# A two-direction Mamba block: groups of 128 channels over all 1024 tokens, one ring of ten slots written in place, and a second set of states prepared by token

## The reference, cut to what matters

```python
xz = einsum(h, W_in); x, z = halves          # 256 channels each
x = silu(causal_conv(x, 4 taps) + conv_b)
dt, B, C = split(einsum(x, Wx))              # rank 64, 16 states, 16 states
dt = softplus(einsum(dt, Wdt) + bdt)
dA = exp(dt * A)                             # token x channel x state
dBx = (dt * x) * B
h_t = dA_t * h_(t-1) + dBx_t ; y_t = sum over states of h_t * C_t
y = (y + x * D) * silu(z); out = einsum(y, W_out)
```

## Time and profile before

| what | value |
|---|---|
| runs | 877.89 and 879.49 us |
| span of the profiled execution | 875.2 us, so 2.7 to 4.3 us of a run's time lie around a span |
| DVE busy | 796.6 us, 91% |
| POOL busy | 794.2 us, 91% |
| ACT busy | 654.4 us, 75% |
| PE matmul busy | 644.4 us, 74% |
| mean granted TensorE clock | 0.878 |
| moved | 108.12 MB, mean 124 GB/s |

### The profile page before, as it was taken

The page is one execution under the profiler, slowest core; times in us unless marked ns, Lnnn a source line. Parts: engine busy times, 40 slices in busy tenths (PEclk is TensorE's granted clock), DMA queues, the critical chain, the costliest instruction groups (busy, mean ns, idle before and its releaser), DMA issues. The chain is left out here.

```text
span 875.2 us, 9930 instructions
## 1 busy us (share of the span) xinstructions
PE 644.4 (74%) x2650; PEld 262.4 (30%) x2650; DVE 796.6 (91%) x816; ACT 654.4 (75%) x1147; POOL 794.2 (91%) x391
## 2 busy tenths in 40 slices
PE   8577786967778795867787795878788696568474
PEld 5232231413333231313333231323333131223223
DVE  3379999999999999999999999999999999999866
ACT  3588787877879787876888787876888786865514
POOL 0398999999998999999998999999998999998925
PEclk9989796979989798979889798989989897966778
DMA  3885746474765745583775656484675557385003
GB/s 68 173 191 108 160 97 144 87 160 79 174 137 121 168 88 119 97 185 76 153 163 109 152 93 135 84 190 93 130 162 107 121 104 154 75 180 181 25 0 97
DMA packets 82103, 108.12 MB, mean 124 GB/s; under 512 B 43648, under 2 KB 56960, under 8 KB 81792
## 3 DMA queue, kind: packets, MB, share of 16 engines
q1 hardware_dynamic: 82048, 107.49, 57.6%
...
## 5 line engine op out<-in xcount | busy, mean ns | idle before, releaser
L582 POOL TENSOR_TENSOR dbx<-step_rep,bc_rep 128x1024 f32<-128x1024 f32 x192 | 452.5, 2379 | 14.6 <-DMA step_rep<-step 12.1
L835 ACT ACTIVATE da_ps<-step_rep,neg_a 128x512 f32<-128x512 f32 x384 | 257.7, 690 | 95.5 <-DVE hs L1109 94.5
L592 POOL TENSOR_TENSOR ch<-hs,bc_rep 128x1024 f32<-128x1024 f32 x120 | 284.9, 2375 | 19.9 <-DVE hs L1109 15.3
L1109 DVE TENSOR_TENSOR_SCAN hs<-da_ps,dbx 128x512 f32<-128x512 f32 x192 | 220.5, 1204 | 24.4 <-ACT da_ps L835 12.0
L1109 DVE TENSOR_TENSOR_SCAN hs<-da_ps,carry,dbx 128x512 f32<-128x512 f32 x192 | 232.6, 1264 | 5.9 <-ACT da_ps L835 5.9
L1369 PE MATMUL y_ps<-ch,stack 128*32 128x512 f32 x1024 | 158.1, 693 | 91.4 <-POOL ch L592 53.2
L761 ACT ACTIVATE dbx_tok<-c_ps,b_cols 128x256 f32<-128x256 f32 x256 | 111.0, 489 | 27.2 <-PE c_ps L1421 22.4
L1360 PE MATMUL c_ps<-x_dbl,select 128*128 128x512 f32 x160 | 105.2, 745 | 33.7 <-DVE ch L1020 27.0
L1020 DVE TENSOR_TENSOR ch<-hs,c_ps 128x2048 f32<-128x2048 f32 x56 | 126.6, 2261 | 0.0
L1308 PE MATMUL pre<-h_t,w_conv 128*128 128x512 f32 x248 | 113.6, 600 | 7.5 <-ACT xs L713 5.8
L1433 PE MATMUL da_ps<-ident,dbx_tok 128*128 128x128 f32 x512 | 76.6, 284 | 33.6 <-DVE hs L1109 32.4
...
## 6 DMA issues: line engine op xcount, KB each, us to landing
step_rep<-step SPq DMA_DIRECT2D x256, 256.0 KB, 5.4
...
```

Of the source, the lines that this page charges most:

```text
L582: nc.gpsimd.tensor_tensor(dbx[:, j % DBX_RING], dtx_rep[:, r], b_rep[:, s % 2, k, :].unsqueeze(1).to_broadcast([P, 2, CHUNK]), ALU.mult).t ...
L592: nc.gpsimd.tensor_tensor(ch[:, n % RING], hs[:, n % RING], c_rep[:, s % 2, k, :].unsqueeze(1).to_broadcast([P, 2, CHUNK]), ALU.mult).then ...
L835: nc.scalar.activation(bank, dt_rep[:, r, e, :], ACT.Exp, scale=neg_a[:, half_of(unit), 2 * (unit % 2) + e, g, k:k + 1]).then_inc(da_ready, 1)
L1109: nc.vector.tensor_tensor_scan(in_scan_order(hs[:, n % RING, e, :], s), in_scan_order(factor, s), in_scan_order(term, s), initial, ALU.mul ...
```

## The change

A group is now **128 channels of one direction over all 1024 tokens**. The scan of a unit is one instruction of 128 x 1024 instead of two of 128 x 512, and starts from zero: there is no kept state. There are again 4 groups for each batch and 16 units in a group, four **places** of four units, one place for each quad. A direction is two groups. This text numbers the units of a direction 0 to 31: 0 to 15 are its first ("even") group, 16 to 31 its second ("odd") one.

`ring` has ten slots of 128 x 1024. A slot holds `dBx` (or, for a unit by token, the decay), then the scan's result, then the product with C, all in place. A slot is free again when PE has summed the whole place of its last unit (`wait_slot`). PSUM has two sets of 1024 columns (`SETS = 2`, `s_ps`) in place of three banks of 512.

By token are now units 12 to 15 and 16 to 19 (quad 3 for both groups, `scale_both`, 32 instructions of 256 columns for each direction, as many as before) and units 28 to 31 (quad 2 of the odd group, `scale_one`, 32 instructions of 128 columns, new). B by token is turned round on PE (`turn_b`); the small transfers are gone. POOL makes C products for units 8 to 19 and 28 to 31, DVE for 0 to 7 and 20 to 27, as two instructions of 4 x 512 columns for each place (`times_c`): one after the place's last scan, one after the scan behind it.

```diff
-RING = 4
+RING = 10
+SETS = 2
-B_AHEAD = 3
-DA_BANKS = 3
-STATE_QUADS = (((0, 1, 2, 3), (0, 3, 1, 2)),) * NG
-TOKEN_QUADS = ((3,),) * NG
-DA_SLOTS = 4
-DBX_RING = 4
-POOL_C = ((0, 1, 3, 8, 9, 12, 13),
...
+QUADS = ((0, 1, 2, 3), (3, 0, 1, 2))
+TOKEN_PLACES = ((3,), (0, 3))
+POOL_C_PLACES = ((2, 3), (0, 3))
...
+CONVOLVE = {0: (0, 5, 7, 11), 2: (3, 5, 8, 11)}
+SILU_AT = 13
+X_DBL = (14, 15)
+SOFTPLUS_AT = 7
+DTX_AT = (8, 9)
...
+EXPS_AFTER = ((2, 3, 4, 5, 6, 7, 8, 9, 10, 11, 13, 14, 15, 16, 17, 18),
+              (3, 4, 5, 5, 6, 7, 8, 9, 10, 11, 13, 14, 15, 16, 16, 17))
+B_FIRST = 2
+B_AFTER = ((3, 4, 5, 6, 7, 9, 10, 11, 12, 12, 12, 12, 12, 12, 13, 13),
+           (1, 2, 2, 3, 4, 5, 6, 7, 8, 8, 8, 8, 9, 9, 10, 10))
+BOTH_TAKEN = (14, 1, 5, 9)
+BOTH_SCALED = {(1, 15): (0, 0, 4), (0, 0): (0, 4, 8), (0, 1): (1, 0, 4), (0, 2): (1, 4, 8),
+               (0, 5): (2, 0, 4), (0, 6): (2, 4, 8), (0, 9): (3, 0, 4), (0, 10): (3, 4, 8)}
...
+            def scan(b, s, n):
+
+                i = unit(b, s, n)
+                dve.wait_ge(da_ready, i + 1)
+                slot = ring[:, i % RING, :]
+                factor, term = s_ps[:, i % SETS, :], slot
+                if by_token(s, n):
+                    dve.wait_ge(dbx_ps, tokens_turned(b, s, n) + 1)
+                    factor, term = slot, factor
...
+            def turn_tokens(b, s, n):
...
+                pe.wait_ge(scanned, i - SETS + 1)
```

More of the change, by code:

```diff
@@ L22 @@
 FAR = QUAD // NEAR
-UNITS = STATES // QUAD * INNER // BLOCK // 2
-TRANSPOSE_REV, COPY_REV = (4, 5), (5, 6)
-FIRST_STAGES = {"silu": 10, "x_dbl": 13}
-LATER_STAGES = {"copy x_dbl": 0, "u0": 1, "u1": 2, "take u0": 2, "take u1": 3, "softplus": 5, "dtx": 7}
-CONVOLVE = (7, 7, 8, 8)
-CONVOLVE_READ = 8
-PROJECTIONS = {"z0": 6, "z1": 6, "z2": 3, "z3": 6, "h0": 3, "h1": 4}
-PROJECTIONS_READ = {"z0": 6, "z1": 6, "z2": 5, "z3": 7, "h0": 4, "h1": 6}
-CLOSING = {"save": 3, "start sum": 3, "gate": 2, "output": 4, "residual": 5, "mean": 6, "deviation": 6,
-           "scale": 8, "keep": 9, "transpose": 10, "affine": 13, "largest": 15}
@@ new lines, in take_step @@
+            def take_step(d, j):
+                place, c = j // 2, j % 2
+                g = d % 2
+                a = half_at(g, place)
+                wait_filled(act, "step", d, j)
+                if j == 0:
+                    for r in range(BLOCKS):
+                        act.wait_ge(dt_in[r], FAR * 16 * 2 * d)
+                    wait_dtx(act, d - 1, 1)
+                nc.scalar.activation(step[:, a, 0, columns(c)], pre[:], ACT.Identity, bias=bdt[:, g, a:a + 1]).then_inc(pre_taken, 1)
@@ L692, in copy_z, with softplus @@
+            def softplus(d):
+                nc.scalar.preload_act_table_set(SOFTPLUS)
+                for place in range(2):
+                    wait_taken(act, "step", d, 2 * place + 1)
+                    part = step[:, half_at(d % 2, place), 0, :]
+                    nc.scalar.activation(part, part, ACT.Softplus).then_inc(dt_ready, 1)
+                nc.scalar.preload_act_table_set(EXP)
             def copy_z(b, j):
                 a, c = divmod(j, CHUNKS)
-                if j == 0 and not (isinstance(b, int) and b == 0):
-                    act.wait_ge(o_ps, CHUNKS * b)
@@ L894, in _ @@
+            for j in range(2 * CHUNKS):
+                a, c = divmod(j, CHUNKS)
+                act.wait_ge(u_first_ps, j + 1)
+                bank = (s_ps[:, 0, CHUNK:SEQ], s_ps[:, 1, 0:CHUNK], y_ps[:, 0, :], y_ps[:, 1, :])[j]
+                nc.scalar.activation(step[:, a, 0, columns(c)], bank, ACT.Softplus, bias=bdt[:, FWD, a:a + 1]).then_inc(dt_first, 1)
             nc.scalar.preload_act_table_set(EXP)
@@ L901, in _ @@
             act.wait_ge(cols_in, 16 * 4)
[L902 to L911 removed]
+            exponential(0, 0, 0)
@@ L1151, in _ @@
[L1151 to L1157 removed]
+            dve.wait_ge(dt_first, 2)
+            dve.wait_ge(xs_first, 3)
+            nc.vector.tensor_tensor(step[:, 0, 1, :], step[:, 0, 0, :], xs_of(0, 0), ALU.mult).then_inc(first_dtx, 1)
+            dve.wait_ge(a_ps, 1)
@@ new lines, in add_units @@
+            def add_units(b, s, p, c):
+                if by_pool_c(s, p):
+                    pe.wait_ge(ch_pool, pool_c(b, s, p * BLOCKS + BLOCKS - 1) + 1)
+                else:
+                    pe.wait_ge(ch_vector, vector_c(b, s, p, c) + 1)
+                for r in range(BLOCKS):
+                    i = unit(b, s, p * BLOCKS + r)
+                    ins = nc.tensor.matmul(y_ps[r * BLOCK:(r + 1) * BLOCK, c, :], stack[:], ring[:, i % RING, columns(c)],
+                                           start=False, stop=p == PLACES - 1 and s != 1)
+                ins.then_inc(summed, 1)
```

1829 lines of the change are left out of this document (911 added, 918 removed), and 3 rows, old and new, of the table EXPS_AFTER.

## The result

The changed kernel takes **1014.0 us** (1010.3 and 1017.7) against 878.7: a ratio of 1.156, 95% interval 1.143 to 1.168. 915 was forecast, with a range up to 938. (Times here are medians; one execution of the later kernel f1 took 1977.5 us, twice its three others, for a reason that I don't know, and is in none of them.) The direction was right, the size was not: of 135 us lost, the forecast had 36. The profiled execution took 1010.3 us with a span of 1008.5; 912 was forecast for it, so 96.5 us of span are missing from the forecast.

What follows compares the result with a forecast made beforehand. POOL and DVE's ring of waits bounds the kernel: 82.9 start, 7 x 97.5, 34.8, 28.6, closings 19.2, PE and ACT 25 put the last scan at 873; with 38.7, span 912, a run 915 us, range 868 to 938.

Steps and rivals of the forecast that it cites:

- Prices: Start to start: POOL product 2.32 us, scan 2.21, C product of 2048 columns 2.18, scaling 0.43 or at most 0.41.
- Start and end: First product at 41.8 us, scan 9 of the first direction done at 82.9; 38.7 after the last scan.
- The loop by its order: POOL and DVE waiting on each other in order: 97.5 us a direction, 195 a batch, 201.4 with closings.
- steps 1, 3 and 4: One direction: scan 9 to B 23, 34.8 us; C 29 to B 2, 11.6; scans 2 to 9, 26.4.
- the 3.1 for PE and ACT: Share of one direction, in scan 9 to scan 23, of the 25 us forecast for PE and ACT.
- step 2: Scans 23 to 29 with four C products on DVE: 24.2 us, POOL running out of work.
- PE and ACT on the same ring: Units 8 to 13: PE and ACT make C 13 start 2.7 or 3.9 us late; 25 us in all.
- three terms left: Turning tokens behind the sum at unit 1, PE clock below mean, 128-column scalings ahead of DVE's C product: left at nothing.
- amounts decide: Rival: POOL's and DVE's smaller amounts of work set the loop, batch 186.4 us, end near 830; chance 0.09.
- POOL and DVE alone: Rival: the order of POOL and DVE costs what was forecast, PE and ACT hide: 890 us; chance 0.25.
- the fourth: Rival: ACT and PE bind in the odd group too, about 930 to 940 us; chance 0.22.
- three signs of being wrong: Scan of 1024 far from 2.2; no DVE wait for L626 in odd group; first scans before 40 us.

Runs made afterwards that it cites:

- f1: e1 with B products earlier in POOL's order, and dtx and dt replication ahead of the third B rows and the closing's stores; 980.2 us, ratio 1.117.
- e6: e1 plus only taps 0 and 3 in the loop, one scaling in four from the second batch, earlier dtx and dt replication (other outputs); 921.3 us, 1.049.
- e1: Changed kernel with PE's turns of units 1, 5 and 9 in even groups issued ahead of the rest of their unit; 941.9 us, 1.071.
- h1: Changed kernel with only the turn of unit 1 moved ahead of the rest of its unit; 972.0 us, 1.104.
- h2: Changed kernel with only the turns of units 5 and 9 moved ahead of half convolutions and sums; 975.0 us, 1.108.
- e4: Changed kernel with the next group's dtx and dt rows ahead of B rows and closing's stores in SP's queue, odd groups; 997.6 us, 1.135.
- f3: e1 with the convolution's last piece one unit earlier in even groups, and earlier replication of dtx and dt; 943.1 us, 1.074.

## Why the prediction was wrong

- **Prices**: right. POOL's two C products of 4.65 us together are followed by the next product 4.61 after their start, 2.31 each, a scan 2.19 to 2.21, a C product of 2048 columns 2.18 to 2.21. In-place writing shows no price (2363 and 2367 ns a product, 2379 and 2375 before). With their small gaps the scans of the loop average 2.24, about 1 us a direction above the forecast's 2.21. The scalings were dearer in the forecast than on the chip: five of 128 columns take 1.41 us below, the last about 0.41 of it, so 0.25 from start to start. That is the Trainium skill's estimate ("VectorE: DVE Perf Modes", the section on the TRN2 errata); my 0.41 came from four normalisations in 1.65 us, which are another operation on another tile, and whose last duration counts in full. It changed little, since the forecast's path has only scalings of 256 columns (four in 1.59 here, 1.72 in the forecast).

```profile
473.13 1.41 ACT L835 ACTIVATE tok<-c_ps,b_cols 128x128 f32<-128x128 f32 x5 [0.28 <-PE c_ps L1434]
```

- **Start and end**: right within 4 us. The first product starts at 41.63 (41.8 forecast), the end after the last scan is 38.2 (38.7). Scan 9 of the first direction ends at 86.8 for 82.9: scan 3 starts at 60.0, some 1.3 late, and 2 us are the same PE and ACT waits at units 7 to 9.

```profile
41.63 2.35 POOL L626 TENSOR_TENSOR ring<-dtx_rep,b_rep 128x1024 f32<-128x1024 f32 x1 [8.35 <-DMA dtx_rep<-step]
```

- **The loop by its order** (POOL and DVE, 97.5): right in its steps 1, 3 and 4, within 1.0 us each in e6 (step 1 is 36.4 there without the 3.1 for PE and ACT). The waits stand where it put them, 2.6 to 3.1 for 2.8 before scan 2, and in e6 6.8 for 6.6 from unit 12 to scan 23; POOL's before L635 too. It is short by 3.7 us a direction in e6, 2.3 of them in step 2, at the late C broadcasts.
- **PE and ACT on the same ring**: this step failed. It followed one passage, units 8 to 13, for 3.3 us a direction. That passage was sized about right: from scan 9 to scan 23 the table has 40.0 us in e1 for 39.5, and the 2.7 more of the changed kernel go with the turns. (Its 2.9 for the second direction isn't the sum of its terms, 1.0 + 0.6 + 1.8, which is 3.5 with the hand-over; that is 0.3 us a direction.) What it lacks are the same kind of passage at units 1, 5 and 9: 9.1 us of waits at units 3 to 11 for none. Of the three terms left "at nothing, each some 1 us a direction", the turn of tokens behind the sum at unit 1 alone was worth 42 us (h1), and the same passage at units 5 and 9 39 us (h2). So that term, put at some 1 us a direction and then at nothing, measures about 5 (42 / 8). I sized it by the sum that stands in front (1 to 2 us), not by what all stands behind: four scalings, an exp that a scan wants, and the C broadcast. I also took PE's durations from a stretch at full clock (1.00 granted from 500 to 530 us of the kernel before); behind a wait of 8 us the sum took 3.64 instead of 1.85, and 0.826 was granted on the mean, 0.878 before.
- **The transfers between directions**, in no part of the forecast: e4 measures 16 us, most of it through the late turn, since f3 has nothing of it left. In the queue's rows SP issues the closing's store as soon as ACT has made its tile, and then 16 replications, with ACT's exp waiting until 627 for the first dt rows:

```profile
608.19 0.33 SPq L532 DMA_DIRECT2D xn_rows<-xhat  x1
608.61 1.16 SPq L484 DMA_DIRECT2D b_rep<-bc_rows  x2
609.87 8.33 SPq L459 DMA_DIRECT2D dtx_rep<-step  x8
618.30 9.17 SPq L459 DMA_DIRECT2D dt_rep<-step  x8
```

- **The rivals**: "amounts decide" is refuted by POOL at 73% of the span, where that rival was to show 98% in a batch; "POOL and DVE alone" was 31 us short even where PE and ACT were relieved (e6); the fourth named PE and ACT, but in the odd group. That came as well, but at step 2 it is 2.2 us a direction of the 13.2 that are missing. I had no rival in which the even group's first half binds, and 0.22 was all that lay beyond the forecast. None of my three signs of being wrong came up either: a scan costs 2.2, DVE waits for L626 in the odd group, and the first scan comes at 44.1.

Of the 63 us between e1 and the kernel before, 36 are the forecast's own, and 7 x 3.6 = 25 are what a direction of e1 (107.4) has over the forecast's 103.8, most of it in step 2. Open is how much of this is PE's clock: I found no way to raise it without other work on PE.
